# The causal mask of the second local tile: from a TensorE pass to a VectorE addition

## The reference, cut to what matters

```python
remote = Tq - LW                       # 1024 - 256
pool = lambda a: concat([a[:, :, :remote].reshape(..., nblk, MB, d).mean(3), a[:, :, remote:]], axis=2)
k_pos = jnp.concatenate([jnp.arange(nblk) * MB + (MB - 1), jnp.arange(remote, Tq)])
scores = (q_sem . k_sem2) / sqrt(32) + (q_geo . k_geo2) / sqrt(32)
scores = scores * jnp.exp(logit_scale)[None, :, None, None]
mask = k_pos[None, :] <= pos[:, None]
scores = jnp.where(mask[None, None], scores, NEG_INF)     # NEG_INF = -1e9
probs = softmax(scores); out = probs @ v2; out @ Wo
x = layernorm(x + attention(x)); x = layernorm(x + ffn(x))
```

## Time and profile before

| | |
|---|---|
| median of 3 runs | 1614.06 us (1612.95 to 1615.53) |
| the profiled execution's own time | 1613.25 us |
| its span, first to last instruction | 1611.5 us |
| TensorE busy in the span | 96% |
| VectorE busy in the span | 65% |
| ScalarE busy in the span | 38% |
| mean granted TensorE clock | 0.989 of full speed |

### The profile page before, as it was taken

The page is one execution under the profiler, slowest core; times in us unless marked ns, Lnnn a source line. Parts: engine busy times, 40 slices in busy tenths (PEclk is TensorE's granted clock), DMA queues, the critical chain, the costliest instruction groups (busy, mean ns, idle before and its releaser), DMA issues.

```text
span 1611.5 us, 28943 instructions
## 1 busy us (share of the span) xinstructions
PE 1540.3 (96%) x10280; PEld 1385.8 (86%) x10280; DVE 1039.5 (65%) x1771; ACT 616.2 (38%) x1257; POOL 463.7 (29%) x584
## 2 busy tenths in 40 slices
PE   6999999999998599999999999999999999999996
PEld 5987987888887488889999989999998999999995
DVE  6865766776675588875576466566466557557544
ACT  4163254245235444433333333343333333333322
POOL 5474355456446433420030030030040022003001
PEclk9999999999999799999999999999999999999999
DMA  7031022122221677568667667767776857766861
GB/s 266 16 136 42 21 92 86 35 79 99 68 79 46 255 280 294 223 254 294 226 232 280 230 221 264 265 219 243 277 244 205 302 208 249 280 241 213 285 230 58
DMA packets 92089, 307.76 MB, mean 191 GB/s; under 512 B 9888, under 2 KB 10272, under 8 KB 90144
## 3 DMA queue, kind: packets, MB, share of 16 engines
q1 hardware_dynamic: 90928, 301.54, 53.3%
q10 hardware_dynamic: 1008, 4.20, 0.6%
HBM read 255.37 MB, written 50.33 MB: 190 GB/s over the span
## 4 chain that ended last, share of the span: by engine, by line
PE 60%; DVE 4%; issue 2%; ACT 0%; POOL 0%; DVEq 0%; POOLq 0%; ACTq 0%
PE ff_bank_b L1755 16%; PE ff_bank_a L1755 10%; PE ff_bank_c L1755 10%; PE ff_acc L94 7%; PE ff_acc L96 7%; PE ff_acc L95 7%; DVE ff_d_lo L1569 1%; PE ff_x_ps L1726 1%; PE ff_x_ps L1708 1%; DVE ff_x_lo L1554 1%; DVE ff_ring L1559 0%; PE ff_x_ps L1716 0%; PE ff_x_ps L1717 0%; DVE ff_c L1615 0%; DVE ff_bn L1691 0%
## 5 line engine op out<-in xcount | busy, mean ns | idle before, releaser
L1755 PE MATMUL ff_bank_b<-ff_x_hi,ff_ring 128*128 128x256 f32 x1536 | 305.3, 281 | 8.0 <-DVE ff_c L1609 5.1
L1755 PEld LDWEIGHTS ff_bank_b<-ff_x_hi,ff_ring 128*128 128x128 f32 x1536 | 249.7, 189 | 13.4 <-DVE ff_ring L1559 7.1
L1755 PE MATMUL ff_bank_b<-ff_x_lo,ff_ring 128*128 128x256 f32 x768 | 215.4, 280 | 0.0
L1755 PE MATMUL ff_bank_a<-ff_x_hi,ff_ring 128*128 128x256 f32 x1024 | 205.2, 283 | 10.4 <-issue 7.9
L94 PE MATMUL ff_acc<-ff_d_hi,ff_h_hi 128*128 128x512 f32 x512 | 203.8, 398 | 2.7 <-DVE ff_d_lo L1569 2.7
L1755 PE MATMUL ff_bank_c<-ff_x_hi,ff_ring 128*128 128x256 f32 x1024 | 205.4, 283 | 0.0
L96 PE MATMUL ff_acc<-ff_d_hi,ff_h_lo 128*128 128x512 f32 x512 | 199.7, 390 | 0.0
L95 PE MATMUL ff_acc<-ff_d_lo,ff_h_hi 128*128 128x512 f32 x512 | 199.4, 389 | 0.0
L1755 PEld LDWEIGHTS ff_bank_a<-ff_x_hi,ff_ring 128*128 128x128 f32 x1024 | 166.4, 189 | 11.4 <-issue 8.7
L1755 PEld LDWEIGHTS ff_bank_c<-ff_x_hi,ff_ring 128*128 128x128 f32 x1024 | 165.9, 189 | 2.2 <-issue 1.7
L1609 DVE TENSOR_TENSOR ff_c<-ff_bank_b,ff_c 128x512 f32<-128x512 f32 x64 | 44.2, 690 | 173.6 <-PE ff_bank_b L1755 173.6
(11 more groups left out here) (306 smaller groups left out, 3515.6 us busy)
## 6 DMA issues: line engine op xcount, KB each, us to landing
ff_ring<-gu_scratch SPq DMA_DIRECT2D x392, 512.0 KB, 5.0
gu_scratch<-ff_ring SPq DMA_DIRECT2D x56, 512.0 KB, 3.8
at_xt<-in_xt SPq DMA_DIRECT2D x4, 2048.0 KB, 8.0
at_xn<-in_x SPq DMA_DIRECT2D x32, 256.0 KB, 2.9
x_scratch<-at_x SPq DMA_DIRECT2D x32, 256.0 KB, 2.0
ff_raw<-in_wgu SPq DMA_DIRECT2D x8, 1024.0 KB, 6.4
at_wd_a<-in_wd SPq DMA_DIRECT2D x8, 512.0 KB, 4.4
mixed_scratch<-at_wd_a SPq DMA_DIRECT2D x8, 512.0 KB, 3.1
```

What stands on the lines that cost most here:

```text
L1755: i = pe.matmul(bank[:, m, :], r[:, a, m, c, :], b[:, k, c, :], start=(k < 3 and m == 0 and c == 0 and b is x_hi and a == 0), stop=(m == 1 ...
```

## The change

The mask pass (L1072) is issued only for tt = 0. For tt = 1, VectorE adds the mask table to the last 128 key columns of both heads of a pair, in place in PSUM, before it takes the maximum, and waits for its own addition on a new semaphore `lmasked`. The eight semaphores of the output weights' pieces become one: ScalarE now waits for the sum of all eight before it converts the first piece.

```diff
-        wq_in, wo_in = [sem(f"wq_in{c}") for c in range(DC)], [sem(f"wo_in{c}") for c in range(8)]
+        wq_in, wo_in = [sem(f"wq_in{c}") for c in range(DC)], sem("wo_in")
...
+        lmasked = signal("lmasked", 8)
...
             for c in range(8):
-                sp.dma_start(wo_raw[c], io["wo"][:, c, :]).then_inc(wo_in[c], 16)
+                sp.dma_start(wo_raw[c], io["wo"][:, c, :]).then_inc(wo_in, 16)
...
             for c in range(8):
-                act.wait_ge(wo_in[c], 16)
+                act.wait_ge(wo_in, 16 * 8)
                 act.activation(wo_hi[:, c, :], wo_raw[c], ACT.Copy).then_inc(wo_hi_s, 1)
...
                         dve.wait_ge(*ls_ps.now(b, 8 * tt + p + 1))
                         pair = pair_scores(tt, p)
+                        if tt:
+                            dve.tensor_tensor(pair[:, :, keys - P:keys], pair[:, :, keys - P:keys], bc(causal, 1, 2), ALU.add).then_inc(lmasked.sem, 1)
+                            dve.wait_ge(*lmasked.now(b, p + 1))
                         dve.tensor_reduce(stat[:, tt, 0, 2 * p:2 * p + 2], pair[:, :, 0:keys], AX.X, ALU.max, negate=True).then_inc(lmax.sem, 1)
...
                             pe.matmul(out, u, kt_hi[:, a, s, 0:keys], start=True, stop=False)
-                            pe.matmul(out[:, keys - P:keys], ident_r[:, :], causal_r[:, :], start=False, stop=False, skip_group_check=True)
+                            if tt == 0:
+                                pe.matmul(out[:, keys - P:keys], ident_r[:, :], causal_r[:, :], start=False, stop=False, skip_group_check=True)
```

More of the change, by code:

```diff
@@ L627, in _ @@
             prime(dve, xsum, xpool_s, krope, v_lo_s, kr_s, kt_lo_s, bd_s, vbd_s, vb_lo_s, vwo_lo_s, qrope,
-                  masked, shifted, summed, probs_s, pt_lo_s, added, bn_s, qt_lo_s, lmax,
+                  masked, shifted, summed, probs_s, pt_lo_s, added, bn_s, qt_lo_s, lmasked, lmax,
                   lrecip, tp_lo_s, o_lo_s)
```

## The result

The changed kernel takes 1620.44 us in the median of 14 executions, the kernel before, timed beside it, 1615.93 us. The ratio is 1.0033 (95%: 1.0021 to 1.0044), so the change costs 5.3 us (3.4 to 7.1); the difference of the medians is 4.5. The forecast was 1621.5 us, in the range 1615 to 1627. The profiled execution's span is 1621.2 us, 9.7 more than that of before, its own time 1623.02 us.

A forecast was written before the change was run, and what follows sets the result against it. The prediction took TensorE's local rounds to be held by a VectorE-ScalarE chain. Delays of 1.1 + 4.4 + 2.2 = 7.7 us raise the profiled 1613.25 to 1621.0; with the run median 0.8 higher it forecast 1621.5 us, range 1615 to 1627.

The forecast's parts named there:

- What bounds the kernel: Local rounds: TensorE is busy 96%, but stands tenths of a microsecond behind a VectorE-ScalarE chain, which the change lengthens.
- The rival in which TensorE stays the bound: Local rounds: VectorE's added work is covered, so the removed passes gain 5.8 us, giving 1608.3; chance 0.08.
- The addition: VectorE, each of 32 pairs: 0.42 us for 256 elements, bounds 0.29 and 0.69; 0.46 with the wait.
- The round's delay and rounds 5 and 6: Second pair's chain 0.63 us later each round; round 5's gain gone; in round 6 TensorE newly waits for ScalarE.
- Round 7 and the batches 0 to 2: Maxima 1.58 us late in round 7; next batch's keys 1.47 late after 0.57 slack; three batches, 4.4 us.
- these 0.31 swallow a part: Round 7: VectorE's 0.21 wait before the residual plus a 0.10 gap absorb part of the 1.89 us lateness.
- The last batch: L851 of round 7 is 2.2 us late, and all behind it; up to 1.7 more clock loss for the range.
- The start: ScalarE's first conversion waits 1.4 us for the last weight piece; less 0.3 cover, 1.1 us, range 0 to 1.4.
- "The feed-forward block as long as before.": Expected sign in the changed kernel's profile: the feed-forward block's length does not change.
- Rival (b): Delays partly given back by unfound slack at batch borders, start free: sum between -3 and +3, about 1615; chance 0.15.
- The sum: Whole kernel: 1.1 start + 4.4 batches 0 to 2 + 2.2 last batch = 7.7 us slower.
- Rival (c): VectorE's PSUM write is dear, or new waits lower TensorE's clock every batch: 12 us or more, about 1629; chance 0.10.

The follow-up runs named there:

- Run 3: Kernel before with the second tile's mask pass taken out and nothing in its place, leaving that tile unmasked; 1609.56 us, 0.9966.
- runs 6 and 11: Run 6 has its own line; run 11: mask on VectorE, early semaphores, two of eight additions a batch issued earlier, plus 64 idle VectorE increments; 1615.93 us, 1.0003.
- run 1: Kernel before with only the eight output-weight semaphores made one, the mask staying on TensorE; 1616.95 us, 1.0028.
- run 9: Kernel before with 64 idle TensorE increments behind the attention, plus the single output-weight semaphore; 1613.30 us, 0.9986.
- run 6: Kernel before with 64 idle semaphore increments behind TensorE's last attention instruction, nothing else; 1611.66 us, 0.9980.
- run 2: Against the kernel before, only the mask addition moved to VectorE, with seven early output-weight semaphores instead of one; 1618.47 us, 1.0025.
- the padded kernels: Kernels with idle semaphore increments behind the attention: 64 on TensorE (1612.42, 1611.66, 1625.02, 1613.30 us), 32 or 64 on VectorE (1614.26, 1615.93 us).
- runs 1 to 4: Start alone, mask alone, no second-tile mask, and mask alone with the addition twice; timed beside the kernel before (median 1614.17 us): 1616.95, 1618.47, 1609.56, 1638.79 us.

## Why the prediction was right, point by point

**What bounds the kernel.** Right. Run 3 shows it most clearly: with the pass gone and nothing in its place, TensorE's local rounds gain 2.3 of the 7.7 us, because the chain over VectorE and ScalarE stands right behind it. The rival in which TensorE stays the bound and gains 5.8 us in the local rounds falls.

**The addition.** Forecast 0.42 us by the line between two rows, measured 0.42. The trace of before had a nearer row than the two, and the prediction passed it over: VectorE's low parts of the remote probabilities (L646) are one subtraction over 256 elements, from PSUM into SBUF, 422 ns in the mean of 32. Here it is in the list of that trace's groups of instructions, shapes kept apart (before the bar the count, behind it busy us, mean ns of one, and idle us before them):

```profile
L646 DVE TENSOR_TENSOR at_pt_lo<-at_mid,at_pt_hi 104x256 fp32r<-104x256 f32 x32 | 13.5, 422 | 27.6 <-ACT at_pt_hi L484 27.6
```

Beside it, the write to PSUM costs nothing of its own. As estimates from the Trainium skill, "VectorE: DVE Perf Modes", section on the TRN2 errata, an fp32 addition of 256 elements takes 424 ns by its formula for SBUF and 392 ns by its cycle table for a PSUM source; the trace, with both a PSUM source and a PSUM result, agrees with the first (415 to 423 ns), and so does L646.

**The round's delay and rounds 5 and 6.** The second pair's exponentials were forecast at 2.30 behind the first addition and stand at 2.29. In round 6 TensorE was to become late by about 1.05; it was 5.86 - 4.77 = 1.09. The wait of round 5 falls on the low part of the probabilities (L829), as the forecast's round 5 has it; its round 7 does not name the same wait there (0.47).

**Round 7 and the batches 0 to 2.** Forecast 1.47 each, measured 1.71. The step that was mis-sized is "these 0.31 swallow a part": VectorE was to lose its pause before the residual. It did not. TensorE's tile is done well before the residual there (its last pass starts at 129.25, the residual at 130.88), and still VectorE pauses for 0.37 us, put down to issue: the 0.21 of the earlier trace rows was not a wait for TensorE alone. The addition of group 7 starts 134.32 - 127.73 - 4.77 = 1.82 late, almost the full 3 x 0.63 = 1.89, and the first pair's exponentials end 2.28 late instead of 2.04. Less the slack of 0.57 that is 1.71.

**The last batch.** Forecast 2.2, measured 1.8; the wait before the output is 3.39, 1.0 longer, and the rest went into waits of 0.6 and 0.75 ahead of it. VectorE's L851 shows where the 0.4 went. From round 3 on it falls behind by 0.57, 0.57, 0.10 and 0.53 in rounds 4 to 7, together 1.77; in batch 0 these were 0.63, 0.62, 0.61 and 0.60. Each round delay is smaller by some 0.06, and in round 6 a pause is swallowed after all: before, L851 waited there for ScalarE's L603, and in the changed kernel it does not. First before, then after:

```profile
508.39 0.68 DVE L851 TENSOR_TENSOR at_qo_lo<-at_tr,at_qo_hi 64x512 fp32r<-64x512 f32 x1 [0.26 <-ACT at_qo_hi L603]
```
```profile
520.11 0.65 DVE L855 TENSOR_TENSOR at_qo_lo<-at_tr,at_qo_hi 64x512 fp32r<-64x512 f32 x1
```

The clock behind the wait before the output is not lower than before (0.65 in 527 to 531, with 0.56 in the earlier trace rows), so the second loss of 1.7 that was kept for the range did not come.

**The start.** Forecast 1.1 for the wait, measured 1.5. The cover of 0.26 was there. The mis-sized term is VectorE's move: its rotation starts 1.45 late, but its copies end 1.74 late, because one instruction of the rotation (L654 before, L655 after) takes 0.95 us instead of 0.67; 1.74 less the cover is 1.47. The size also rests on two traces. In the ten traces of kernels with early semaphores TensorE starts these transposes between 37.05 and 38.63 us, the kernel before at 37.24; in the three with the single semaphore between 38.71 and 39.24. The means are 1.2 us apart.

What was not priced is the clock behind the wait. Stretches of lower clock between 38 and 58 us stand in all three traces with the single semaphore (3.4, 1.7 and 1.7 us of full speed lacking), and in two of the ten without it (runs 6 and 11, 1.7 each). Three comparisons of times give the start's whole cost: run 1 against before (+4.5, by the medians +2.8), run 9 against run 6 (+1.0 to 1.6), and after against run 2 (1.0033 and 1.0025, +1.3), each uncertain by some 2 us. In all three the mean granted clock of the timed executions is lower with the single semaphore: 0.9867 and 0.9879, 0.9879 and 0.9891, 0.9876 and 0.9885 (standard errors of the differences 0.0006, 0.0003, 0.0005). Within the kernels here 0.001 of mean clock goes with 1.3 us, so this would be 1.2 to 1.6 us. The wait and this clock loss together would be about 3 us; two of the three comparisons show no more than the wait. So the wait is shown, and a clock loss of about a microsecond behind it is likely but not shown: it is a correlation, and no run held the clock fixed.

**"The feed-forward block as long as before."** Wrong, and the one step that failed in kind. It was 2.6 us shorter (2.9 in run 2), and the padded kernels show that differences of this size come without any change to addition or pass, from where the code behind them lies. Rival (b), the delays partly given back, was right in that something is given back, but it named the batches' borders, and the borders give back nothing.

**The sum.** Forecast 6.6 + 1.1 = 7.7 us; measured in the trace 6.9 + 1.5 in the attention, less 2.6 behind it: 5.8, beside a clock loss of 3.3 that is larger in this execution than on average. The timed 5.3 fits that, as far as a single trace can tell. That the forecast of 1621.5 came only 1.1 us above the median is partly luck. As a difference it was 7.4 us, above the measured 5.3 and its interval of 3.4 to 7.1; it stood on a median before that was 1.9 us lower than that of the later 14 executions. And it has errors that partly cancel: too little for the start and for batches 0 to 2, too much for the last batch, nothing for the give-back. The mechanism of the local rounds, and its size of 6.9 with 6.6 forecast, is what it had right.

**Rival (c)**, a dear write or a clock pulled down in every batch, falls on both counts: 0.42 us, and no lower clock behind the waits of the local rounds in batches 0 to 2.

**A faster version.** Run 6, the kernel before with 64 idle increments, is faster than both kernels: 0.9980 (0.9972 to 0.9989). It was found by chance and is no design: the next edit ahead of the loop moves the code again.

## What to carry to other kernels

Before a pass is moved from the busiest engine to one with room, follow the chain of waits at that place: here TensorE was busy for 96% of the span, and taking 7.7 us of passes from it was worth 2.3 us even with nothing in exchange, while 0.46 us more on a chain link cost 0.63 a round. Where an experiment deletes instructions, run it also with as many idle ones in their place or behind them: 64 of them moved this kernel by -3 to +7 us, as much as the change under study, and about half of the 7 was clock. And when eight waits are made one, the first consumer pays for the last piece.

## What the hardware showed that was not expected

- **The place of code.** TensorE's time at the turns of a long loop depends on what lies ahead of it in the code: 64.1 to 69.0 us for the same two turns, all at full clock, and kernels with their code at the same place agree to 0.4 us over the block. VectorE's does as well: with 32 increments ahead, an idle time of 5.18 us put down to issue and two waits of TensorE of 2.5 us are gone. The runs show the dependence and its place, not its cause and not the rule by which a place is good; that the engine goes back to code that must be brought in again is my reading of "issue", not shown.
- **The clock.** Stretches at a lower granted clock come also without a wait ahead of them. In run 6, which has no wait at the start, TensorE is busy without a pause in these windows and in the two before them (38 to 46 us), and the clock is between its two levels of 1.2 and 2.4 GHz:

```profile
46.00:50.00 4.00, 4.00 (x19) 0.64 0.00 0
50.00:54.00 4.00, 4.00 (x17) 0.93 0.00 0
```

Such stretches lie elsewhere in other executions, and they are most of what differs between executions of one kernel: of the executions of before beside runs 1 to 4 the fastest took 1611.14 us at a mean clock of 0.990, the slowest 1617.87 at 0.986.
